# Cross attention with the query weights folded into the keys: scores straight from the normed rows

## The reference

```
h = layernorm(x);  x = self_attention(h) + x                  # 16 heads of 64
h = layernorm(x);  x = cross_attention(h, ctx) + x            # 16 heads of 64, ctx is (2, 77, 192)
h = layernorm(x);  x = (a * gelu(gate)) @ ff_w2 + b2 + x

cross_attention: q = h @ wq (256 x 1024); k = ctx @ wk; v = ctx @ wv (192 x 1024)
                 softmax(q k^T / 8) over the 77 keys of each head; times v; @ wo + bo
```

## Time and profile before

| | |
|---|---|
| Runs of the kernel before | 1806.38, 1812.54, 1818.61 us; median 1812.54 |
| The profiled execution's own time | 1805.41 us |
| Its span | 1803.7 us |
| PE, DVE, ACT, POOL busy, share of the span | 91%, 64%, 59%, 53% |
| Mean granted clock of TensorE | 0.976 of full speed |
| `ca0` | 830.2 to 998.8 us of the span |

### The profile page before, as it was taken

One profiled execution on the slowest core, in us unless ns is written; L12 is line 12 of the kernel. 1 busy time (PEld: TensorE's weight loads), 2 busy tenths in 40 slices (PEclk: granted clock), 3 DMA queues, 4 the chain that ended last, 5 costly groups with the idle time before them and its releaser, 6 DMA issues. The chain is left out here.

```text
span 1803.7 us, 28397 instructions
## 1 busy us (share of the span) xinstructions
PE 1647.8 (91%) x9636; PEld 1037.0 (57%) x9636; DVE 1158.9 (64%) x2021; ACT 1062.6 (59%) x1394; POOL 963.0 (53%) x734
## 2 busy tenths in 40 slices
PE   6789999999999999888999889997899988898799
PEld 3445544444444444386666778884444436565579
DVE  7557677777777777385777843347778754776513
ACT  4556678888888888743554533311676763454452
POOL 1456688888889888861222620201334443466405
PEclk9999999999999999998999999996899999999899
DMA  2010121111111111030000010102334321000101
GB/s 97 24 35 31 35 68 36 42 35 62 37 41 35 41 35 48 12 106 27 1 1 1 13 33 24 30 13 52 90 72 100 78 64 42 9 1 1 36 15 48
DMA packets 54313, 70.93 MB, mean 39 GB/s; under 512 B 18176, under 2 KB 41884, under 8 KB 54207
## 3 DMA queue, kind: packets, MB, share of 16 engines
q1 hardware_dynamic: 54207, 69.54, 13.7%
HBM read 41.72 MB, written 2.37 MB: 24 GB/s over the span
## 5 line engine op out<-in xcount | busy, mean ns | idle before, releaser
L1694 POOL TENSOR_TENSOR x<-x,sa_p_buf 128x1024 f32<-128x1024 f32 x190 | 453.6, 2387 | 126.9 <-ACT sa_p_buf L1430 114.1
L1562 DVE TENSOR_REDUCE sa_mx<-sa_front 128x1 f32<-128x512 f32 x512 | 327.4, 681 | 106.5 <-PE sa_front L1285 104.9
L1430 ACT ACTIVATE sa_p_buf<-sa_score 128x1024 f32<-128x1024 f32 x256 | 249.3, 1024 | 130.8 <-PE sa_score L1322 130.6
L1341 PE MATMUL sa_out<-sa_p_buf,sa_v_buf 128*64 128x512 f32 x1024 | 246.4, 602 | 0.0
L607 ACT ACTIVATE sa_p_buf<-sa_score 128x1024 f32<-128x1024 f32 (+1 forms) x160 | 140.6, 943 | 75.0 <-PE sa_score L555 74.9
L402 DVE TENSOR_REDUCE sa_mx<-sa_front 128x1 f32<-128x512 f32 (+1 forms) x224 | 136.4, 651 | 31.2 <-PE sa_front L316 27.6
L2287 POOL TENSOR_TENSOR x<-x,bias_out 128x1024 f32<-128x1024 f32 x24 | 61.6, 2581 | 163.1 <-POOLq L2615 141.1
L2154 POOL TENSOR_TENSOR ca_probs<-ca_s_sb,ca_inv 128x616 f32<-128x616 f32 x64 | 78.1, 1220 | 121.6 <-DVE ca_inv L2069 121.6
L1285 PE MATMUL sa_front<-sa_k_hi,sa_q_hi 64*128 64x512 f32 x512 | 117.0, 453 | 22.2 <-DVE sa_mx L1562 17.1
L1341 PEld LDWEIGHTS sa_out<-sa_p_buf,sa_v_buf 128*64 128x64 f32 x1024 | 64.5, 136 | 123.5 <-issue 97.4
L1440 ACT ACTIVATE sa_score<-sa_m_all 128x1024 f32<-128x1024 f32 x128 | 130.8, 1034 | 0.6 <-DMA sa_m_all<-sa_m_line 0.6
(11 more groups left out here) (254 smaller groups left out, 3547.1 us busy)
## 6 DMA issues: line engine op xcount, KB each, us to landing
sa_m_all<-sa_m_line SPq DMA_DIRECT2D x16, 512.0 KB, 3.6
x<-sa_m_line SPq DMA_DIRECT2D x16, 512.0 KB, 4.3
sa_v_buf<-o SPq DMA_DIRECT2D x15, 512.0 KB, 5.0
x<-in_x SPq DMA_DIRECT2D x8, 512.0 KB, 5.8
sa_q_stack<-sa_hi SPq DMA_DIRECT2D x32, 128.0 KB, 2.6
sa_k_stack<-sa_hi SPq DMA_DIRECT2D x32, 128.0 KB, 2.6
sa_recip<-sa_den_out SPq DMA_DIRECT2D x32, 128.0 KB, 2.7
ff_w<-in_L_xattn_ff_w SPq DMA_DIRECT2D x16, 128.0 KB, 2.2
```

Source lines behind the costliest of these rows:

```text
L1341: mm = pe.matmul(out_ps[64 * j:64 * j + 64, :], v_buf[:, b, kt, 64 * j:64 * j + 64], p_buf[:, s % NPB, j, :], start=(kt == 0), stop=(kt == ...
L1430: nc.scalar.activation(p_buf[:, s % NPB], score_ps[s % len(score_ps)][:], ACT.Exp, scale=SCALE).then_inc(exp_done, G)
L1562: dve.tensor_reduce(mx[:, b, j, qt, half:half + 1], front_ps[bank(item, j)][:], AX.X, ALU.max).then_inc(drained, 1)
L1694: nc.gpsimd.tensor_tensor(acc[:, h], prev, cur, ALU.add).then_inc(added, 1)
```

## The change

`ca0` is made by a new function, `folded_attention`; `decoder_blocks` calls it in the place of the old one. The second block's cross attention stays. A score is h wq_h k_h^T; before, h wq_h was made for every row. Now wq_h k_h^T is made once for every head and batch, as M (256 x 77 per head and batch), and the score is h M.

- Opening: PE turns the query weights (16 transposes, in two halves), makes the keys of each pair of heads, and folds: for each of eight pairs two fp32 matmuls (one per 128 rows of the model's width) of 308 columns (2 batches x 2 heads x 77) into a pair of PSUM banks. ACT copies the high part to `m_hi`, DVE the low part to `m_lo`. Turned weights and spread keys lie in the last columns of `oT`, which the stage's output fills only later.
- A unit is now one token tile and eight heads: again 32 units of 128 x 616 scores. `score` is twelve fp32r matmuls of 308 columns: two halves of width, three products of parts, two halves of the eight heads (one bank each). The stationary operand is the tile's rows. `query` and its copy are gone.
- `take`, `exponent`, `invert`, `scale`, `turn`, `evict` handle as many columns as before. `weighted` runs once for two units: eight fp32 matmuls of 256 columns. Its result (two banks, `o_ps`) is copied by ACT (`store`) and not by DVE.
- Lags: TensorE's slot is `score(n)`, `turn(n-3)`, `weighted(n-4)` in every other slot; `store` at n-5.
- `probs` and `v_all` use the memory of `wk` and `wq`, which POOL clears once they have been read.

```diff
-                    cross_attention(nc, "ca0", wide, hT, ctxT, ident, kv, {}, oT, loads)
+                    folded_attention(nc, "ca0", hT, ctxT, ident, kv, oT, loads)
...
+        wq_turned = oT[:, :, (CH - 1) * HALF:(CH - 1) * HALF + D]
+        keys = oT[:, :, (CH - 2) * HALF:(CH - 2) * HALF + B * PK]
+        m_bank = [s_ps[0], s_ps[1], s_ps[0], s_ps[1], t_ps, o_ps, t_ps, o_ps]
+        v_bank = [t_ps[:, 0, :], t_ps[:, 1, :], o_ps[:, 0, :], o_ps[:, 1, :]]
...
+                def fold(p):
+                    pe.wait_ge(wq_set, p // GP + 1)
+                    pe.wait_ge(k_set, 2 * GP if m_bank[p] is o_ps else p + 1)
+                    if p % GP >= 2:
+                        pe.wait_ge(m_split, p - 1)
+                    for k in range(KD):
+                        mm = pe.matmul(m_bank[p][:, k, 0:B * PK], wq_turned[:, p, k * P:(k + 1) * P], keys[:, p, :],
+                                       start=True, stop=True)
+                    mm.then_inc(m_full, 1)
...
+                def score(n):
...
+                    if n >= 2:
+                        pe.wait_ge(s_taken, n - 1)
+                    at = slice(tile(n) * P, (tile(n) + 1) * P)
+                    parts = [(hs, ms, k) for k in range(KD) for hs, ms in ((h_hi, m_hi), (h_hi, m_lo), (h_lo, m_hi))]
+                    for i, (hs, ms, k) in enumerate(parts):
+                        for h in range(2):
+                            k0 = g * KEYS + h * HK
+                            mm = pe.matmul(s_ps[n % 2][:, h, 0:HK], hs[:, c % 2, k, at], ms[:, k, b, k0:k0 + HK],
+                                           start=(i == 0), stop=(i == len(parts) - 1))
+                    mm.then_inc(s_full, 1)
...
+                def turn(n):
...
+                    pe.wait_ge(scaled, n + 1)
+                    if n:
+                        pe.wait_ge(t_done, n)
+                    else:
+                        pe.wait_ge(v_set, 2)
+                    for h in range(GH):
+                        mm = pe.transpose(t_cols[:, h * P:(h + 1) * P], probs[:, n % 2, h, :], ident[:])
+                    mm.then_inc(t_full, 1)
...
+                def weighted(n):
+                    if not unit(n) or n % PAIR != PAIR - 1:
+                        return
...
+                    for p in range(GP):
+                        for j in range(2):
+                            mm = pe.matmul(o_cols[dh * j:dh * j + dh, p * PAIR * P:(p + 1) * PAIR * P],
+                                           v_all[:, group(n) * GP + p, batch(n), j, :],
+                                           turned[:, q % 2, 2 * p + j].rearrange("p u t -> p (u t)"),
+                                           start=True, stop=True, skip_group_check=True)
+                    mm.then_inc(o_full, 1)
...
+                turn_weights(0)
+                keys_of(0)
+                for p in range(GP):
+                    fold(p)
+                turn_weights(1)
+                keys_of(1)
+                score(0)
+                fold(GP)
+                score(1)
+                for p in range(GP + 1, PAIRS):
+                    fold(p)
+                for i in range(NV):
+                    values_of(i)
+
+                def slot(n):
+                    if n >= 2:
+                        score(n)
+                    turn(n - T_LAG)
+                    weighted(n - O_LAG)
...
+            @block.scalar
...
+                    if n >= 3:
+                        exponent(n - 1)
+                    evict(n - T_LAG)
+                    store(n - C_LAG)
+                    if coming_rows(n) is not None:
+                        rows_high(coming_rows(n))
...
+            @block.vector
...
+                for p in range(GP):
+                    keys_of(p)
+                rows_low(0)
+                for p in range(GP):
+                    folded_low(p)
+                for p in range(GP, PAIRS):
+                    keys_of(p)
+                take(0)
+                folded_low(GP)
+                take(1)
+                folded_low(GP + 1)
+                invert(0)
+                folded_low(GP + 2)
+                folded_low(GP + 3)
+                dve.wait_ge(cleared, 1)
+                for i in range(NV):
+                    values_of(i)
+                rows_low(1)
...
+                    if n >= 2:
+                        take(n)
+                        invert(n - 1)
+                    if coming_rows(n) is not None:
+                        rows_low(coming_rows(n))
```

250 lines of the change are left out of this document (added).

## The result

The changed kernel took 1787.53 us (median of four, 1784.49 to 1787.69) against 1813.92 for the kernel before in the same series: a ratio of 0.9864, 95% interval 0.9843 to 0.9886. Two later series gave the unchanged kernel after 0.9895 (0.9866 to 0.9924) and 0.9878 (0.9852 to 0.9904). Over all series, 50 executions of before have the median 1809.9 (1805.5 to 1818.6) and 14 of after 1788.0 (1784.5 to 1801.8): 21.9 us less, 1.2%. One further execution of before, 2098.8 us at a mean granted clock of 0.742, is in none of these figures. The first series had drawn a high median of before. The forecast was 1794 in a range of 1784 to 1806, by a saving of 18.5.

The account below looks back on a forecast made before the run. TensorE's stream was taken to bound the first cross attention; opening 30.8, steady part 105.2 and tail 13.2 gave 149.2 us, 19.4 less, cut to 18.4 for the opening's clock. From the median 1812.5 that gave 1794, range 1784 to 1806.

Parts of the forecast that it names:

- TensorE's stream sets the stage: First cross attention: TensorE runs without pause while other engines wait, so what is taken from its stream is taken from time.
- A unit of 3.69: Steady part after the change: score 1.90, turning 0.85 and weighted sum 0.94 us of TensorE per unit, against 4.47 before.
- The two changes between fp32 and fp32r: TensorE, around each score: switching number format costs 0.11 us in and 0.09 back, raising the score from 1.70 to 1.90.
- The opening, 30.8: Stage start: turning query weights, keys, eight folds, two scores and values, with the clock rising at 836.2; third score starts at 30.8 us.
- The microsecond that I had taken off the saving: Opening: 1 us off the saving for a clock no row shows for this order of work, 19.4 to 18.4.
- The tail, 13.2: From the last score's end to the next block: last turns, evictions, weighted groups and copy take 13.2 us against 9.7.
- All fit: Other engines after the change: DVE 2.8 with gaps, ACT 2.25 and POOL about 1.2 us, within a unit of 3.69.
- 0.56 of cover: Slots without weighted sum: the one turning buffer's loop takes 2.19 us against TensorE's turn and score of 2.75.
- (a): Opening and restart of the next block are slower because the clock stays low; saves 11 to 15, giving 1800; chance 0.17.
- (b): Turning buffer decides: ACT's evictions come late in slots without weighted sum, 0.7 us a pair; saves 8, giving 1804; chance 0.10.
- (c): Weight loads don't hide under 308-column score matmuls, each 0.178 us longer; 49 us slower than before, 1862; chance 0.05.
- (d): More is won: opening warms at once and weighted groups' fixed costs fall; saves 22 to 26, giving 1788; chance 0.08.

Follow-up runs that it names:

- store_first: Changed kernel with ACT's output copy placed before the eviction of the turned tiles instead of behind it: 1785.92 us, ratio 0.9863; repeated, 1786.57 us, ratio 0.987.

## Why the prediction was right, and where it was off

**TensorE's stream sets the stage, before and after: right.** Shown from both sides by taking a product from each kernel's stream (4.01 us a unit of the kernel before, where 4.02 was due; 0.86 of 1.13 a pair after), and after by a steady part without a pause. "Without a pause" was read from one unit, and for the whole steady part before it is too strong: the two units in which rows are split took 0.63 more each. The kernel after has no such pause, so 1.3 of its 22.1 us are a wait that went and not stream that was saved. The forecast priced the new stage whole, so this gain is in its sum, but without a name.

**A unit of 3.69: 3.61 measured.** The price of the 308-column matmul was exact. The two changes between fp32 and fp32r were charged at 0.20 a unit and turned out almost free: turn and score together take 2.57, where their columns alone are 0.85 + 1.70 = 2.55 and 0.85 + 1.90 = 2.75 was charged. In the other direction the entry to column halves, 0.17 a group, was not charged. The net is 105.2 forecast and 102.7 measured for the steady part; that it came so close owes something to the two errors having opposite signs.

**The opening, 30.8: 29.3 measured.** TensorE came to 2.4 GHz near 835 (0.75 in the stretch 833 to 837), 5.6 us after its work began and not 6; fold 2 started 8.8 us into the stage (9.25), fold 7 at 21.2 (22.1), the values at 22.7 (23.9). The microsecond that I had taken off the saving for this clock stood on no row, and no run shows it: the opening was 1.5 shorter than the sum without it.

**The tail, 13.2: 14.5 measured.** The step that failed is "its eviction ends at 9.8, the weighted group at 11.75": I had the group wait for its eviction alone, and it also waits for the copy that frees the sums. store_first took out 1.0 of the 1.3. The rest is that the last eviction ended 10.2 us after the last score and not 9.8.

**"All fit": right for the engines' totals, too generous for the turning buffer.** 0.56 of cover was forecast and 0.32 is there. The forecast took turn and score as 2.75, which was 0.18 too long; the rest is in the loop. Nor was the one buffer of sums looked at, and with the copy on DVE it would have cost 5.4 us.

**Rivals.** (a) and (b) were not met: no clock of 0.50 past 837, no TensorE pause before a turn in the steady part. (c) is refuted by the interval 0.142. (d) came nearest in size: 22.1 in the stage, at its lower edge and the forecast's upper, but by neither of its reasons: the opening did not warm at once (0.50 until 835), and the weighted groups' fixed cost rose from 0.16 to 0.33.

**The median.** 18.5 was forecast; 26.4 in the first series, 21.9 over all. The working gave 19.4 and the stage 22.1, an error of 2.7: opening 1.5, steady part 2.5, tail 1.3 the other way. The further 4 us of the first series are before's four executions, whose median is 4 above that of fifty. I had put equal chances on more and less than 1%, and the stage alone is 1.2%.

## What to carry to other kernels

Where one engine's stream sets a stage, price the new stream instruction by instruction between rows of its neighbours in size; that gave this steady part within 2.5%, with two errors that partly cancelled. Then list every buffer with one copy and ask behind what, on the engine that frees it, the freeing instruction stands: all the waits that surprised here were that (the tail, the copy on DVE, the sums for each unit, the two split places of the kernel before), none an engine that was short of time. An engine's total says nothing about it.

## What the runs showed of the hardware

Eight transposes take 0.97 us before a group of matmuls in column halves and 0.80 before plain fp32r matmuls, and the group itself 1.87 where its columns take 1.71. So such a group costs 0.33 us beyond its columns, in front and behind; twice as many groups for the same columns cost 0.36 us more for each group added. The Trainium skill has a rule that bears on it ("TensorEngine Tiling (Array Packing)", Key Properties): a change of tiling mode drains the engine. The rows agree with a price at both borders; they don't show that draining is its cause.

Loads of 128 columns, each recorded as 0.189 us, follow each other every 0.142 us with the fp32r matmuls over them, and don't lengthen that stream by more than 0.014.

Untouched code moves with the clock: the same ten microseconds of one stage, busy 6.9 us both times, ran at a granted clock of 1.00 in one execution and 0.83 in another and got through 40 and 28 matmuls. Fifty executions of one kernel spread over 13 us, the longer ones at the lower mean granted clock (0.977 to 0.969). What decides the clock in such a stretch stays open.
